# Causal attention: the mask of a row tile's maxima added by VectorE in the reduce, or by a TensorE matmul

## The reference, cut to what matters

```python
def _causal_sdpa(q, k, v):
    scores = jnp.einsum('bhqd,bhkd->bhqk', q, k) * scale
    mask = jnp.tril(jnp.ones((Tq, Tq), dtype=bool))
    scores = jnp.where(mask, scores, -jnp.inf)
    probs = jax.nn.softmax(scores, axis=-1)
    return jnp.einsum('bhqk,bhkv->bhqv', probs, v)
...
A1 = _causal_sdpa(q1, k1, v)
A2 = _causal_sdpa(q2, k2, v)
diff = A1 - lam * A2
rms = jnp.sqrt(jnp.mean(diff * diff, axis=-1, keepdims=True) + EPS)
```

## Time and profile before

| | |
|---|---|
| three runs | 1786.18, 1789.22, 1791.82 us (median 1789.22) |
| profiled execution, its time | 1788.79 us |
| profiled execution, its span | 1787.0 us |
| TensorE busy over the span | 1519.5 us (85%) |
| VectorE busy | 1288.3 us (72%) |
| ScalarE busy | 1088.8 us (61%) |
| GpSimd busy | 1095.8 us (61%) |
| exponentials of the first attention (L588) | from 141.0 to 636.0 us |

### The profile page before, as it was taken

How to read it: one execution, slowest core, us unless ns; L and a number is a source line. 1 busy time by engine, 2 the same in 40 slices (tenths; PEclk the granted TensorE clock), 3 DMA queues, 4 the chain that set the end, 5 groups by cost and what they waited for, 6 DMA issues and landing times. The chain is left out here.

```text
span 1787.0 us, 30008 instructions
## 1 busy us (share of the span) xinstructions
PE 1519.5 (85%) x8532; PEld 1025.8 (57%) x8532; DVE 1288.3 (72%) x3447; ACT 1088.8 (61%) x2348; POOL 1095.8 (61%) x1272
## 2 busy tenths in 40 slices
PE   3759999999999836468874899999999999988898
PEld 2413434344443315356653688888788888867565
DVE  5458887888888313755255899999999999983443
ACT  1105666676666721211312799999999999995242
POOL 5211565665647563104234699999999999974353
PEclk9958999999999968789986999999999999999899
DMA  3321011010100001762010000000000000000000
GB/s 118 113 64 36 22 26 29 19 36 18 30 24 20 2 1 47 246 225 95 1 47 0 1 1 2 1 1 1 1 1 1 29 21 1 1 1 1 1 24 24
DMA packets 39162, 59.48 MB, mean 33 GB/s; under 512 B 8700, under 2 KB 33160, under 8 KB 38152
## 3 DMA queue, kind: packets, MB, share of 16 engines
q1 hardware_dynamic: 39048, 58.12, 10.2%
HBM read 40.93 MB, written 16.78 MB: 32 GB/s over the span
## 5 line engine op out<-in xcount | busy, mean ns | idle before, releaser
L1896 POOL TENSOR_SCALAR c_R<-c_Z,c_negtau 128x256 f32<-128x256 f32 x519 | 589.7, 1167 | 51.4 <-DVE c_negtau L1965 29.7
L588 ACT ACTIVATE a_PT<-a_sc 128x512 f32<-128x512 f32 x576 | 318.4, 600 | 209.6 <-PE a_sc L653 207.2
L1851 ACT ACTIVATE c_R<-c_Z,c_negtau 128x256 f32<-128x256 f32 x1017 | 425.9, 517 | 3.5 <-DVE c_negtau L1998 1.8
L493 DVE TENSOR_REDUCE a_mpart<-a_nat 128x1 f32<-128x512 f32 (+3 forms) x640 | 364.0, 628 | 86.3 <-PE a_nat L620 48.1
L1932 DVE BATCH_NORM_STATS2 c_stat<-c_R 128x6 f32<-128x512 f32 x576 | 380.9, 678 | 1.7 <-ACT c_R L1851 1.6
L617 PE MATMUL a_nat<-KS,QS 96*128 96x512 bf16 (+3 forms) x768 | 242.4, 343 | 33.6 <-DMA KS<-qk_parts 23.8
L1768 PE MATMUL c_z<-mem,c_R 128*128 128x256 f32 x1024 | 231.5, 379 | 0.0
L653 PE MATMUL a_sc<-QS,KS 128*128 128x512 bf16 (+3 forms) x768 | 220.3, 330 | 8.3 <-ACT a_PT L588 5.7
L460 POOL TENSOR_SCALAR_AFFINE_SELECT a_PT<-a_PT 128x512 f32<-128x512 f32 x128 | 78.8, 639 | 223.2 <-ACT a_PT L588 223.2
L1768 PEld LDWEIGHTS c_z<-mem,c_R 128*128 128x128 f32 x1024 | 192.9, 190 | 25.4
L1925 DVE MAX8 c_x<-c_Z 128x8 f32<-128x256 f32 x384 | 152.3, 408 | 26.3 <-ACT c_Z L1839 25.8
(11 more groups left out here) (319 smaller groups left out, 2237.7 us busy)
## 6 DMA issues: line engine op xcount, KB each, us to landing
qk_parts<-a_parts SPq DMA_DIRECT2D x4, 1536.0 KB, 5.9
QS<-qk_parts SPq DMA_DIRECT2D x192, 32.0 KB
KS<-qk_parts SPq DMA_DIRECT2D x192, 32.0 KB
made<-m_made SPq DMA_DIRECT2D x24, 256.0 KB, 3.8
mem<-made SPq DMA_DIRECT2D x3, 2048.0 KB, 8.1
X<-in_L_attn_x_dram SPq DMA_DIRECT2D x1, 2048.0 KB, 8.4
ternary<-a_W_T SPq DMA_DIRECT2D x1, 2048.0 KB, 6.3
mem<-in_L_ffn_wq_dram SPq DMA_DIRECT2D x1, 2048.0 KB, 14.3
```

What stands on the lines that cost most here:

```text
L493: dve.tensor_reduce(mpart[:, b, j:j + cnt, i, k0 // 512], src, AX.X, ALU.max).then_inc(s_max, 1)
L588: act.activation(PT[:, n % 3, c, :], sc[:, u % 2, :], ACT.Exp, scale=SCALE0).then_inc(s_exp, 1)
L1851: act.activation(split(i, h) if r < NR else whole(i, h), Z[:, slot(i), h, :], ACT.Relu, bias=threshold(i, r, h)).then_inc(s_ra[r], 1)
L1896: pool.tensor_scalar(split(i, h) if r < NR else whole(i, h), Z[:, slot(i), h, :], threshold(i, r, h), 0.0, ALU.add, ALU.max).then_inc(s_rp ...
```

## The change

In strip units the mask matmul is left out. VectorE's `tensor_reduce` is replaced there by a `tensor_tensor_reduce`, which adds a strip of -1e30 values and zeros (`K.mstrip`, 128x512 fp32, the triangle in its last 128 columns) to the scores, writes the sum back to `nat` and takes the maximum into `mpart`. Its waits go through `hold`. The paired units keep their mask matmuls. GpSimd fills the strip beside the other constants.

```diff
@@ attention_inputs, gpsimd
             c.step(pool.memset(mhalf[:], -0.5))
+            c.step(pool.memset(K.mstrip[:], 0.0))
             c.join()
...
+            pool.affine_select(out=K.mstrip[:, 3 * P:], in_=K.mstrip[:, 3 * P:], compare_op=ALU.is_ge, fill=NEG, base=0,
                                pattern=[[-1, P]], channel_multiplier=1).then_inc(s_ident, 1)
             c.step(pool.memset(VA[:], 0.0))
@@ attention_inputs, tensor
-            pe.wait_ge(s_ident, 3)
+            pe.wait_ge(s_ident, 4)
@@ attention_heads, vector
             def unit_maxima(h, u):
                 b, _, segs, cnt = units[u]
-                dve.wait_ge(s_nat, h.count(NU, u + 1))
+                j, i, k0, w = segs[0]
+                own = cnt == 1 and i * P < k0 + w
+                if own:
+                    hold(dve, s_nat, h.count(NU, u + 1), K.s_held)
+                else:
+                    dve.wait_ge(s_nat, h.count(NU, u + 1))
                 if u == 0 and (not isinstance(h.n, int) or h.n > 0):
 
-                    dve.wait_ge(s_negm, h.count(1))
-                j, i, k0, w = segs[0]
-                src = nat[:, (NU * h.k + u) % 3, 0:cnt * w].rearrange("p (a w) -> p a w", a=cnt)
+                    hold(dve, s_negm, h.count(1), K.s_held)
+                src = nat[:, (NU * h.k + u) % 3, 0:cnt * w]
+                if own:
+                    dve.tensor_tensor_reduce(out=src, in0=src, in1=K.mstrip[:, 512 - w:], scale=1.0, scalar=NEG, op0=ALU.add,
+                                             op1=ALU.max, accum_out=mpart[:, b, j, i, k0 // 512:k0 // 512 + 1]).then_inc(s_max, 1)
+                    return
+                src = src.rearrange("p (a w) -> p a w", a=cnt)
                 dve.tensor_reduce(mpart[:, b, j:j + cnt, i, k0 // 512], src, AX.X, ALU.max).then_inc(s_max, 1)
@@ attention_heads, tensor
-                                    start=True, stop=diag >= w)
-                    if diag < w:
+                                    start=True, stop=diag >= w or cnt == 1)
+                    if diag < w and cnt == 2:
                         ins = pe.matmul(out[:, diag:diag + P], K.ident_bf[:], K.mask[:], start=False, stop=True)
```

More of the change, by code:

```diff
@@ L169, in _ @@
             pool.affine_select(out=K.mask[:], in_=K.mask[:], compare_op=ALU.is_ge, fill=NEG, base=0,
+                               pattern=[[-1, P]], channel_multiplier=1).then_inc(s_ident, 1)
+            pool.affine_select(out=K.mstrip[:, 3 * P:], in_=K.mstrip[:, 3 * P:], compare_op=ALU.is_ge, fill=NEG, base=0,
                                pattern=[[-1, P]], channel_multiplier=1).then_inc(s_ident, 1)
@@ L893, in alloc_attention @@
     K.W_raw = sb("W_raw", [P, 2 * NWG, WG])
+    K.mstrip = sb("mstrip", [P, 4 * P])
     K.s_ffn = ctx.enter_context(nc.semaphore("s_ffn"))
```

## The result

The changed kernel takes 1803.34 us (median of 6, 1800.46 to 1808.46) where the kernel before took 1792.67 beside it on the same chip (6 runs): 1.0069 times as long, 95% interval 1.0051 to 1.0087, slower by 9 to 16 us. The prediction was no change, 1788.8 us, with 1801 as its upper end. The profiled execution took 1800.46 us, its span is 1798.8.

A forecast was written before the change was run, and what follows sets the result against it. VectorE and ScalarE, not nearly full TensorE, were taken to set the pace in much of each head. Steady -1.5, warm-up +0.4 and setup +0.7 us sum to -0.4: 1788.8 us, no change, range 1782 to 1801.

The forecast's parts named there:

- 0.10 us a head, times 14.5 heads: -1.5 us: Steady heads: gain of 0.21 us a head less costs of 0.04 and 0.07, over 14.5 heads.
- Masks, 0.21 us a head: Mask matmuls taken from TensorE: 0.058 at u8, 0.036 at u20 and u33, 0.116 at u34 and u35.
- 0.116 for u34 and u35: Two mask matmuls behind the fourth score tile, right before the values: 2 x 0.058 us gained a head.
- rival 1: All masks on TensorE's path after all: 13.5 us of the steady heads come back, 1776.8 us; chance 0.12.
- (a), 0.058 - 0.04: VectorE-bound stretch, u36 to u8: removing u8's mask gives 0.058 us; new instructions at u0 and u5 cost 0.04.
- y = 0.016: Extra time in us of each new VectorE instruction over the reduce it replaces; range kept 0 to 0.13.
- Rival 2: New instruction costs 0.13 us extra, lengthening VectorE's two bursts: 0.45 us lost a head, 1799.5 us; chance 0.23.
- 3 (1.1): Third rival: new instruction takes two cycles a column, 1.1 us start to start, 1859 us in all; chance 0.07.
- u13's hold, -0.07: Separate wait before u13's instruction makes u16 0.125 us late, less 0.055 slack: 0.07 us lost a head.
- u20 goes at 298.82: just covered: VectorE's backlog of 0.15 us behind u13: u17's reduce, over at 298.61, still ends before u20, so no loss.
- Warm-up, +0.4 for 24 strips: Head 0 and first 16 units of head 1: masks give nothing, 24 strip units cost 0.016 us each.
- Setup, +0.7: GpSimd's start: filling the strip, 0.43 us of columns plus a 0.24 us select, delays VectorE's first normalised tile.

The follow-up runs named there:

- the pads: Kernel before plus 72 or 128 semaphore increments on VectorE ahead of its loop over heads: 1803.04 us (1.0075) with 72, 1791.96 us (0.9997) with 128.
- written-out loop: Changed kernel with VectorE's loop over heads written out, so no backward branch and no separate waits: 1787.98 us, 0.9988 of the kernel before.
- no masks: Kernel before without the mask matmuls of the units of one row tile, causal mask missing from their maxima: 1788.33 us, 0.9986.
- changed waits: Kernel before with the 16 one-tile reduces per head waiting through a semaphore instruction of their own plus increment: 1795.54 us, 1.0019.
- waits, multiply-add on GpSimd: Kernel before with those separate waits and the small multiply-add of the mean squares moved from VectorE to GpSimd: 1789.55 us, 0.9991.

## Why the prediction was wrong

**The step that failed** is the sum: "0.10 us a head, times 14.5 heads: -1.5 us", with nothing for the instruction stream. I took from the order of instructions that the change does what it says, and did not count what it adds to the loop: 96 on a body of 305. The trace of the kernel before held the sign, which I did not look for: no instruction packet passes from 270 to 540 us, so its loop stayed resident and a longer one might not. 12.2 of the lost 14.7 us between first and last negated maxima are this, shown by the pads (72: same loss, no change; 128: no loss) and by the written-out loop (change, no loss). The Trainium skill (Runtime: NRT & Kernel Launch, Instruction fetch mechanics) has the rule: a taken branch to a page that is no longer held waits for its fetch. The trace agrees, at 2.4 to 3.0 us a branch; it differs from the page's blocks of 16 KiB and 256 instructions, since these fetches bring 8.2 KB and come 131 recorded instructions apart.

The other 2.5 us, seen in one ordinary period. Start of ScalarE's exponentials from the negated maxima (us), and how much later each kernel is there than the kernel before:

```
exponential              5th   8th   14th  15th  16th  18th  19th  32nd  36th
kernel before            4.53  7.42 11.68 12.32 13.97 15.05 15.55 28.14 31.33
changed kernel          -0.08 -0.02 -0.10 +0.13 +0.14 +0.19 +0.28 +0.19 +0.19
changed, written out    -0.07  0.00 -0.08  0.00  0.00  0.00  0.00 -0.08 -0.08
no masks                -0.06 -0.06 -0.13 -0.12 -0.04 -0.04 -0.04 -0.13 -0.13
changed waits            0.00  0.00  0.00 +0.11 +0.11 +0.24 +0.38 +0.39 +0.39
waits, multiply-add on GpSimd
                         0.00  0.00  0.00 +0.10 +0.10 +0.10 +0.10 +0.10 +0.10
```

- *Masks, 0.21 us a head*: 0.13 in the period shown. Of it 0.06 stands early in the period, where I had u8's 0.058 (it is there before u8, so not u8's alone), 0.08 to 0.09 where I had 0.116 for u34 and u35. u20 and u33 give nothing. What u13 to u15 gain is given back at the 16th, as said. The bounds that argued against rival 1 held.
- *(a), 0.058 - 0.04*: right, 0.02 in the changed kernel, though by another sum. u0 starts 0.41 us after the negated maxima start, 0.32 before, since its two holds follow one another; I had no term for that, and the wait at u5 is 0.57 us where it was 0.58, instead of growing.
- *y = 0.016*: mis-sized both ways, harmless. The new instruction, each time with the next one ready behind it, of 512 and then 384 columns:

```profile
294.63 0.68 DVE L501 CUSTOM_DVE_ANT_0 a_nat<-a_nat,mstrip 128x512 f32<-128x512 f32 x1
...
295.24 0.59 DVE L501 CUSTOM_DVE_ANT_0 a_nat<-a_nat,mstrip 128x384 f32<-128x384 f32 x1
295.75 0.13 DVE L501 DVE_READ_ACCUMULATOR2_ANT a_mpart<- 128x1 f32 x1
295.75 0.59 DVE L501 CUSTOM_DVE_ANT_0 a_nat<-a_nat,mstrip 128x384 f32<-128x384 f32 x1
```

  0.61 for 512, where I had 0.61, but 0.515 for 384, where a reduce takes 0.465: +0.05. Rivals 2 (0.67 to 0.73) and 3 (1.1) fall. Rival 2's own terms add up to 0.50 a head and 1800.2 us, not 0.45 and 1799.5; nothing rests on it.
- *u13's hold, -0.07*: the mechanism was right, the size was not: 0.11 for the wait alone, 0.16 in the changed kernel from the 8th to the 16th exponential.
- *"u20 goes at 298.82: just covered"*: wrong. I took the instructions of `squares` at fixed lengths. The multiply-add waits for GpSimd's select, and turns 0.1 us of delay into another 0.14 in the changed kernel and 0.27 in that with the waits alone, from the 16th to the 19th exponential. Rival 2 named this place, with another cause.
- *Warm-up, +0.4 for 24 strips*: from the first unit to the first negated maxima 22.78 us against 22.40, so 0.38 for the 16 of head 0.
- *Setup, +0.7*: right in the profile, as these rows against the earlier trace rows show; in the time of the whole kernel not to be told.

```profile
21.01 0.26 POOL L183 TENSOR_SCALAR a_rstd<-a_mv 128x16 f32<-128x16 f32 x1
...
24.39 1.38 DVE L226 TENSOR_SCALAR a_xn<-X,a_mv,a_rstd 128x256 f32<-128x256 f32 x4 [4.89 <-POOL a_rstd L184]
```

Without the fetches the forecast's number would have stood, its sum only in part. By an estimate from the 14.7 - 12.2 above, the changed kernel would be 2.5 us longer from first to last where -1.5 was said, which is still inside the range; the written-out one, which is rid of the separate waits too, is 1.1 us shorter.

## What to carry to other kernels

Count the instructions that a change adds to an engine's loop body, waits and accumulator reads included, and look whether the trace before fetches instructions inside the loop: a loop that just stays resident has a cliff (here 12 us, 0.7%), and code ahead of the loop alone can push it over. A short VectorE instruction that has to wait for GpSimd's selects has no fixed length: a delay of 0.1 us ahead of it came out as 0.3 to 0.4. And a nearly full engine may still give little back: 232 removed matmuls of 0.058 us in the steady heads were worth 1.6 us, since VectorE and ScalarE set its pace there.

## What the runs showed of the hardware

- VectorE kept a loop of 305 or 353 instructions without a single fetch in 270 us, and refetched one of the same 305 that began 72 later: five blocks of 8.2 KB an iteration, and a pause of 2.4 to 3.0 us at each backward branch. The packets of the other instruction queue, q8, are 16 KB (0.84 MB in 51). They are TensorE's: every kernel without the 16 mask matmuls a head has 51 of them, every other 52. None passes from 270 to 540 us, though TensorE's body has 1557 recorded instructions (1653 before).
- A wait on a register's value in a semaphore instruction of its own, with an increment behind it, makes a waiting VectorE instruction start 0.11 us later than one that carries the wait (u13, 0.79 us after VectorE fell idle against 0.68).
- A pause costs TensorE more than its length. The granted clock was 1.00 up to it, fell to 0.50 behind 2.8 us of standing still, and came back some 3.3 us after TensorE had resumed: an estimated 1.6 us on top of 2.5. At the other two branches TensorE stood still for 2.6 and 2.8 us, with the same fall. The 0.97 of the 50 us stretches is this.
